# One batch loop with stages becomes an unrolled pipeline over 64 tiles

## The reference

```python
x = x + _layernorm(_L0_attn_ref(_layernorm(x), ...))
x = x + _layernorm(_L0_ffn_ref(_layernorm(x), ...))
```

```python
scores = jnp.einsum('bqhd,bkhd->bhqk', q, k) / np.sqrt(HD)
scores = jnp.where(causal[None, None], scores, jnp.finfo(scores.dtype).min)
attn = jax.nn.softmax(scores, axis=-1)
...
topv, topi = jax.lax.top_k(probs, K)        # K = 2 of 8 experts per row
a = jax.nn.silu(g) * u                      # g, u: per expert, 256 -> 512
out = jnp.clip(residual + moe_out, -100.0, 100.0)
```

## Time and profile before

| | us |
|---|---|
| median of 3 runs | 4165.04 (4164.26 to 4166.23) |
| the profiled execution's own time | 4157.04 |
| its span | 4155.2 |
| TensorE, VectorE, ScalarE, GpSimd busy | 3078.5, 2298.0, 1675.9, 1106.6 |
| mean granted clock of TensorE | 0.873 of full |
| first turn of the batch loop | 31 to 434 |
| experts and final pass | from 3221.6 to the end |

### The profile page before, as it was taken

One profiled execution on the slowest core, in us unless ns is written; L12 is line 12 of the kernel. 1 busy time (PEld: TensorE's weight loads), 2 busy tenths in 40 slices (PEclk: granted clock), 3 DMA queues, 4 the chain that ended last, 5 costly groups with the idle time before them and its releaser, 6 DMA issues. The chain is left out here.

```text
span 4155.2 us, 54042 instructions
## 1 busy us (share of the span) xinstructions
PE 3078.5 (74%) x17636; PEld 1799.8 (43%) x17637; DVE 2298.0 (55%) x4488; ACT 1675.9 (40%) x3702; POOL 1106.6 (27%) x972
## 2 busy tenths in 40 slices
PE   5588558765965696579657955885587599999991
PEld 3444434343434443443444343444343366666660
DVE  4775567466837672866386557755675122222225
ACT  2456254525542554256335624562455122222223
POOL 6310630072016202420332053106200222222222
PEclk9789789887988898889788988997789799999995
DMA  1000000000000000000000000000000533333335
GB/s 55 11 11 12 22 21 2 13 20 21 2 30 3 21 2 32 0 21 2 32 1 21 2 32 11 12 12 22 11 2 11 185 55 55 55 61 56 55 53 167
DMA packets 85960, 125.57 MB, mean 30 GB/s; under 512 B 11600, under 2 KB 70864, under 8 KB 83664
## 3 DMA queue, kind: packets, MB, share of 16 engines
q1 hardware_dynamic: 59216, 85.40, 6.5%
q0 software_dynamic: 26496, 37.01, 5.0%
HBM read 58.23 MB, written 63.36 MB: 29 GB/s over the span
## 5 line engine op out<-in xcount | busy, mean ns | idle before, releaser
L660 ACT ACTIVATE PR<-SP_ 128x512 f32<-128x512 f32 (+3 forms) x1536 | 693.8, 489 | 457.8 <-PE SP_ L1241 310.9
L925 DVE TENSOR_REDUCE NM<-MX 128x1 f32<-128x128 f32 (+7 forms) x1024 | 733.9, 752 | 231.2 <-PE MX L1210 221.0
L421 POOL DMA_INDIRECT scratch_xs<-FX,SLOT x128 | 123.7, 967 | 1467.1 <-issue 1465.5
L439 POOL TENSOR_TENSOR work<-QK,VS 128x2048 f32<-128x2048 f32 x128 | 466.6, 3670 | 136.4 <-DVE QK L774 136.2
L1238 PE MATMUL SP_<-work,KST 99*128 99x512 bf16 (+3 forms) x1536 | 469.0, 333 | 44.1 <-ACT PR L660 32.2
L1208 PE MATMUL MX<-KST,work 96*128 96x512 bf16 (+3 forms) x1536 | 442.8, 353 | 70.0 <-DVE NM L925 58.5
L1503 POOL DMA_INDIRECT scratch_h<-Y,XG x136 | 210.6, 1548 | 617.1 <-DVE Y L1566 522.9
L1544 DVE TENSOR_TENSOR AG<-UB,SL 128x512 f32<-128x512 f32 x136 | 94.0, 691 | 476.3 <-PE UB L1583 476.3
L1254 PE MATMUL OA<-PR,V 128*32 128x512 f32 (+3 forms) x3072 | 327.3, 498 | 3.3 <-ACT PR L660 3.3
L1521 ACT ACTIVATE SL<-GB 128x512 f32<-128x512 f32 x136 | 81.2, 597 | 602.3 <-PE GB L1583 602.3
L818 DVE TENSOR_REDUCE AT<-work 128x256 f32<-128x4096 f32 x64 | 282.9, 4420 | 2.2
(11 more groups left out here) (253 smaller groups left out, 5092.7 us busy)
## 6 DMA issues: line engine op xcount, KB each, us to landing
XG<-scratch_xs SPq DMA_DIRECT2D x136, 130.0 KB, 2.1
X<-in_L_attn_x SPq DMA_DIRECT2D x8, 1024.0 KB, 5.6
scratch_x<-X SPq DMA_DIRECT2D x8, 1024.0 KB, 3.9
scratch_h<-A SPq DMA_DIRECT2D x8, 1024.0 KB, 3.9
X<-scratch_x SPq DMA_DIRECT2D x16, 512.0 KB, 4.0
HH<-scratch_h SPq DMA_DIRECT2D x16, 512.0 KB, 4.5
out<-X SPq DMA_DIRECT2D x16, 512.0 KB, 3.1
wg<-in_L_ffn_Wg SPq DMA_DIRECT2D x1, 4096.0 KB, 16.7
```

Source lines behind the costliest of these rows:

```text
L439: sg["prod1"].by(pool.tensor_tensor(P1[t % 2][:, i * hh * D:(i + 1) * hh * D].rearrange("p (h e d) -> p h e d", h=hh, e=HD), QK[:, t % 3, ...
L660: sg["exp"].by(act.activation(PR[:, n % 8, q0:512], SP_[:, n % 2, q0:512], ACT.Exp))
L925: sg["mx"].by(dve.tensor_reduce(NM[:, qt, h:h + 1], src, AX.X, ALU.max, negate=True))
```

## The change

The loop and the meeting points are gone. Each engine's program is one unrolled list: 87 periods after a short lead-in, 24 slots in each. In period p, slot i, an engine does one step of the front stages for tile p, or p - 1, p - 2, p - 6, p - 7, p - 8, and of the closing stages for tile p - 17 to p - 22. Between these, `share(p, i)` deals out steps of the second attention, from period 12 on: 32 per period in four periods, then 16 per period in four, and so on. The attention's own order (chunks of queries, one after the other over all batches, with a table of maxima in units of a quarter step) is a generator that each engine resumes.

With it, buffers get smaller: tiles of one batch become rings (x 10 tiles, AT 3, A2 6, HS 12), most work tiles single. PSUM is dealt out anew: GA, GB and SUM are one bank each, shared by all front and closing steps; scores keep two banks, maxima have a ring of two, in which the turned output also takes its place. A row maximum over more than 512 keys is now two pieces and two reductions. Key products, query products and query sums are halved (8 heads each). The copy of the attention's output (OT) moves from VectorE to ScalarE. Roots and reciprocals are one power on GpSimd. Norm coefficients are computed per tile, routing per four tiles (it was eight), x is loaded per tile. At the end the program clears its semaphores.

The diff, cut to its core:

```diff
+RX = 10
+RAT = 3
+RA2 = 6
+RHS = 12
+RK = 3
+RV = 4
...
-        XN = sb("XN", [P, 2, D])
-        XT = sb("XT", [P, 2, FC, P])
-        EX = sb("EX", [P, 2, 2 * D])
-        QK = sb("QK", [P, 3, 2 * D])
-        VS = sb("VS", [P, 2, D])
-        SQ = sb("SQ", [P, 2, D])
+        XN = sb("XN", [P, D])
+        XT = sb("XT", [P, FC, P])
+        EX = sb("EX", [P, 2 * D])
+        QK = sb("QK", [P, 2, 2 * D])
+        VS = sb("VS", [P, D])
+        P1 = sb("P1", [P, 2, H * D // 2])
+        P2 = sb("P2", [P, H * D // 2])
+        KT = sb("KT", [P, D])
+        SQ = sb("SQ", [P, D])
+        AT = sb("AT", [P, RAT, D])
...
-        MX = ps("MX", [P, 2, 2, 512])
         SP_ = ps("SP_", [P, 2, 512])
+        GA = ps("GA", [P, 512])
+        GB = ps("GB_", [P, 512])
+        SUM = ps("SUM", [P, 512])
         SP_ = ps("SP_", [P, 2, 512])
+        MX = ps("MX", [P, 2, 512])
         OA = ps("OA", [P, 512])
...
+                first = FIRST_STEP[u]
+                if g == 0:
+                    late = (2.8, 1.6)[c]
+                    spans = [(first - (9, 6.5)[c], first - late)] * 3 + [(first - late, first - 0.8)]
+                    done = first - 0.8
+                else:
+                    done = first - (2.0, 3.0)[c]
+                    begin = max(FIRST_STEP[HKV * j] - 0.6, done - (4, 9)[c])
+                    spans = [(begin, done)] * CH
...
+        SLOTS = 24
+        START = 12 * SLOTS + 4
+        LAST_PERIOD = TT + 23
+        LAST_BACK = TT + 12
+        def share(p, i):
+            if p * SLOTS + i < START:
+                return 0
+            n = 32 if p % 8 < 4 else 16
+            return (i + 1) * n // SLOTS - i * n // SLOTS
...
-            with sp.Fori(0, B - 1) as b:
-                batch(b, True)
+                    do(pool.tensor_tensor(xco[:, 1:2], xco[:, 0:1], powers[:, 0:1], ALU.pow))
...
+                    if t >= 1:
+                        need("heads_summed", 2 * t - 1 + half)
+                    hh = H // 2
+                    r = slice(half * hh * HD, (half + 1) * hh * HD)
+                    sg["prod1"].by(pool.tensor_tensor(
...
-                        sg["ot"].by(dve.tensor_copy(OT[:, :], OA[:, :]))
+                        sg["ot"].by(act.activation(OT[:, :], OA[:, :], ACT.Copy))
...
+                def query_products(t, half):
+                    need("kv", t + 1)
+                    need("attn", 2 * t + half)
+                    r = slice(half * hh * HD, (half + 1) * hh * HD)
+                    sg["prod2"].by(dve.tensor_tensor(
+                        products, QK[:, t % 2, r].rearrange("p (h e) -> p h e", e=HD).unsqueeze(2).broadcast_to(shape),
+                        KVP.rearrange("p (d e) -> p d e", e=HD).unsqueeze(1).broadcast_to(shape), ALU.mult))
+                def query_sums(t, half):
+                    need("prod2", 2 * t + half + 1)
+                    if t >= RAT and half == 0:
+                        need("a2", t - RAT + 1)
+                    r = slice(half * hh * HD, (half + 1) * hh * HD)
+                    sg["attn"].by(dve.tensor_reduce(AT[:, t % RAT, r].rearrange("p (h d) -> p h d", d=HD), products, AX.X, ALU.add))
...
-                for t in range(NT + 3):
-                    if t < NT:
-                        elu(t)
-                    if 2 <= t <= NT + 1:
-                        attended(t - 2)
+                        if i == 0 and have(p - 1):
+                            query_sums(p - 1, 1)
+                        if i == 1 and have(p - 8):
+                            parts(p - 8, 0)
+                        if i == 2 and have(p):
+                            elu(p)
+                        if i == 2 and have(p - 8):
+                            parts(p - 8, 1)
+                        if i == 3 and have(p - 8):
+                            parts(p - 8, 2)
...
+                            flatten(p - 17)
+                        if i in (20, 22) and have(p):
+                            query_products(p, (i - 20) // 2)
+                        if i == 21 and have(p):
+                            query_sums(p, 0)
+                        if p * SLOTS + i == START:
+                            next(back)
+                        for _ in range(share(p, i)):
+                            next(back, None)
...
+                def bank_b():
+                    need("fT", sg["tpf"].n)
+                    need("vcopy", sg["qkv"].n // 2)
+                    need("hT", sg["tph"].n)
...
+                    j, g, c = unit(u)
+                    if index >= 2:
+                        need("mx", index - 1)
+                    need("qts", 2 * (CH * j + i + 1) - (1 if h + G * g < 8 else 0))
+                    need("kts", CH * j + i + 1)
+                    n = min(512, (CH * c + i + 1) * P - 512 * part)
+                    keys = j - c + part
+                    last = part == c
+                    out = MX[:, index % 2, 0:n]
+                    m = pe.matmul(out, QST[0:MROW, j % 2, g * G + h, i * P:(i + 1) * P], KST[0:MROW, keys % RK, g, 0:n],
...
+                for p in range(-1, LAST_PERIOD):
+                    for i in range(SLOTS):
+                        if i == 0 and have(p - 18):
+                            transpose_flat(p - 18)
+                        if i in (1, 2) and have(p):
+                            project(p, i == 2)
+                        if i == 4 and have(p - 18):
+                            route(p - 18)
...
+                        if i == 20 and have(p):
+                            turn_sums(p)
+                        if p * SLOTS + i == START:
+                            next(back)
+                        for _ in range(share(p, i)):
+                            next(back, None)
```

More of the change, by code:

```diff
@@ L162, in attention_kernel @@
+        cmv = sb("cmv", [P, 2])
+        cco = sb("cco", [P, 2, 8])
+        MS = sb("MS", [P, H])
+        R16 = sb("R16", [P, 2, H])
+        row = sb("row", [P, 3])
+        rms = sb("rms", [P, 3])
+        LG = sb("LG", [P, CH, E])
+        top = sb("top", [P, CH, 8])
+        topi = sb("topi", [P, CH, 8], U32)
         below = sb("below", [P, P])
@@ L287, in dve_plan @@
-        def dve_plan():
-            plan = max_plan()
-            yield from plan[0]
-            for k, (u, kt) in enumerate(steps()):
-                actions = plan[k + 1]
-                first = len(actions) // G
-                yield from actions[:first]
-                if kt == 0 and u >= 1:
-                    yield "out", u - 1
-                yield from actions[first:]
-                if kt == 1 and u >= 1:
-                    yield "ctx", u - 1
-            yield "out", len(UNITS) - 1
-            yield "ctx", len(UNITS) - 1
@@ new lines, in attention_kernel, with unit, length, steps @@
+        NU = TT // CH * HKV
+        NSTEPS = TT // CH // 2 * HKV * (CH + 2 * CH)
+        def unit(u):
+            j = u // HKV
+            return j, u % HKV, j % 2
+        def length(u):
+            return CH * (1 + unit(u)[2])
+        FIRST_STEP = [0]
+        for u in range(NU):
+            FIRST_STEP.append(FIRST_STEP[-1] + length(u))
+        assert FIRST_STEP[-1] == NSTEPS
+        def steps():
+            for u in range(NU):
+                for kt in range(length(u)):
+                    yield u, kt
@@ new lines, in last_step, with max_plan @@
+        def last_step(j):
+            return FIRST_STEP[HKV * (j + 1)]
+        def max_plan():
+            timed = []
+            for u in range(NU):
+                j, g, c = unit(u)
[8 more added lines that the diff above has]
+                    spans = [(begin, done)] * CH
+                for i in range(CH):
+                    cells = [("piece", u, h, i, part) for h in range(G) for part in range(c + 1)]
+                    lo, hi = spans[i]
+                    if g == 0 and i == CH - 1:
+                        n0, n1, total = 0, len(cells), len(cells)
+                    elif g == 0:
+                        n0, n1, total = i * len(cells), (i + 1) * len(cells), 3 * len(cells)
+                    else:
+                        n0, n1, total = i * len(cells), (i + 1) * len(cells), CH * len(cells)
+                    for n, cell in zip(range(n0, n1), cells):
+                        timed.append((lo + n * (hi - lo) / total, cell))
+                timed.append((done, ("parts", u)))
+                timed.append((done + 0.3, ("rows", u)))
+                if u >= 1:
+                    timed.append((first + 1.6, ("turn", u - 1)))
+            timed.sort(key=lambda x: x[0])
+            buckets = [[] for _ in range(G * NSTEPS + 1)]
+            index = 0
+            for time, (kind, *args) in timed:
+                at = max(0, 1 + int(time * G)) if time >= 0 else 0
+                if kind == "parts":
+                    buckets[at].append((kind, *args, None))
+                else:
+                    buckets[at].append((kind, *args, index))
+                    index += 1
+            return buckets, index
```

(23 more changed lines are left out.)

1989 lines of the change are left out of this document (988 added, 1001 removed), and 5 rows, old and new, of the table names.

## The result

The changed kernel takes 4242.01 us (median of 4 runs, 4234.28 to 4250.62) beside 4164.94 us of the kernel before on the same chip: ratio 1.0184, 95% interval 1.0172 to 1.0196. It is slower by 1.8%; the forecast was 3790, and 4242 lies above its range (3540 to 4110). The profiled execution has a span of 4235.6 us.

A forecast was written before the change was run, and what follows sets the result against it. First and last stages wait for hand-overs, the second attention for TensorE. Start 29, fill 276, periods 12 to 63 2166, then 310 and 57 sum to 2838; block change 7; experts start 377 us earlier: about 3790 us, range 3540 to 4110.

The forecast's parts named there:

- heavy: Period with 32 steps of the second attention: forecast 47.8 us, with 22.6 us of attention on TensorE.
- light: Period with 16 steps of the second attention: forecast 36.4 us, with 12.7 us of attention on TensorE.
- VectorE's stretch: From VectorE's products in slot 20 to elu of the next tile in slot 2: 15.6 us heavy, 13.1 light.
- The lock: VectorE's cast after elu is held until GpSimd's first product ends: +3.7 us per period, bounds 0 and 7.3.
- The rival without a lock: VectorE's casts and GpSimd's long products pass each other: -192 us, 3600 us; chance 0.22.
- TensorE's stretch: TensorE's work left over after VectorE's stretch, 29.0 and 21.5 us; at 93.9% busy, 30.9 heavy and 22.9 light.
- a head start: TensorE begins its stretch two maximum pieces ahead: -2.4 us in heavy periods, -3.3 in light ones.
- the clock: TensorE, half idle in VectorE's stretch, runs 16 us per period at half speed: +416, about 4205 us; chance 0.13.
- slot-by-slot coupling: TensorE's stretch 80% busy rather than 94%, through waits in 24 slots: +5.4 and +4.0 us, 4030 us; chance 0.14.
- The fill: Periods 0 to 11, without attention: a single-buffered chain per tile of 23 us, 276 us in all.
- The powers: Five GpSimd powers per tile, bounded by 0 and 3.6 us, put at no cost on the path.
- The drain: Periods 64 to 75, without new tiles, TensorE-bound: 310 us; then last four tiles, routing and scatters: 57 us.

The follow-up runs named there:

- the pairs of runs: Heavy periods of three runs, each beside its base kernel: 0.3 to 0.45 us less busy time per us less at the low clock in the middle stretch.
- e13: Changed kernel plus two zero-adding filler matmuls ahead of each maximum piece in slots 20 to 23 and 0 to 5: 4230.83 us against 4242.
- e3: Changed kernel with the logits copy out of bank SUM moved from VectorE to ScalarE: 4153.35 us against 4242.
- e6: Changed kernel with GpSimd's power done for one head root instead of 16, result not valid: 4204.15 us against 4242.
- experiment 5: The same run as e6: changed kernel with GpSimd's power done for one head root instead of 16: 4204.15 us against 4242.
- e14: Kernel with elu behind parts, logits on ScalarE, later second sums, spread products, later norm_heads (3916), plus two zero-adding fillers ahead of pieces: 3936.07 us.
- e10: One filler matmul at the start of slots 20 to 23, 0 and 1, on a kernel with elu behind parts, logits on ScalarE, later second sums (3937): 4004.58 us.

## Why the prediction was wrong

Its sum, term by term, up to the start of the experts:

| | forecast | measured | difference |
|---|---|---|---|
| start | 29 | 31.8 | +3 |
| periods 0 to 11 | 276 | 333.2 | +57 |
| periods 12 to 62 (24 heavy, 27 light) | 2130 | 2453.2 | +323 |
| period 63 to the experts | 410 | 485.9 | +76 |
| experts start | 2845 | 3304.1 | +459 |

**VectorE's stretch** was right: 15.3 + 0.7 for elu = 16.0 us where 15.6 was forecast, light 13.6 beside 13.1.

**The lock** was right in cause and size: the cast is held for 3.67 us, and with the subtraction ahead of it 4.1 us pass from elu's end to its end where 3.7 stood. The Trainium skill, page "SBUF — State Buffer", section "Who interferes with whom", has the second of the two engines held for the whole instruction of the first, and reductions never. The trace agrees with both: the cast takes 3.67 us in 56 of 64 tiles and 0.33 in the last eight, which no product accompanies, and a reduction (L1042) that starts at 1708.49 beside GpSimd's product takes its usual 0.69 us. The rival without a lock falls.

**TensorE's stretch** is the step that failed: "The steady second attention is 93.9% busy at clock 1.00, so 30.9 and 22.9 us", minus 2.4 and 3.3. It came to 34.0 and 25.1 instead of 28.5 and 19.6, +5.5 us in both kinds of period. Its work was right in size: 29.7 busy less 3.6 lost by the clock is 26.1 where 26.6 was forecast, light 18.7 where 18.2. That was partly luck. In VectorE's stretch TensorE did what was forecast (9.0 and 6.6 us at full clock), so its work of a whole period is 35.1 and 25.9 us by the same reckoning, not 38.0 and 28.1; the 2.4 and 3.3 us taken off for a head start, of which the trace shows little (0.0 and 1.1 us busy while the cast is held), made up for it. Two other parts were not right:
- *The clock.* The 1.00 came from a stretch in which TensorE never pauses. In the new order its stretch begins behind a pause, and the earlier trace rows had shown a clock of 0.56 and 0.61 after one. At 3.6 and 2.9 us that is 24 x 3.6 + 27 x 2.9 = 165 us, by the 0.3 to 0.45 of the pairs of runs 100 to 150. That 7.2 and 5.8 us were worked at the low clock is shown; that this much would come back with it is an estimate and not shown, as no run lifted it there alone. Waits that take its place, the rival of e13, are not ruled out.
- *Idle time.* 4.3 and 3.5 us where 6% gave 1.9 and 1.4: 24 x 2.4 + 27 x 2.1 = 114 us. The named part is the wait for the logits copy: taking it away is worth 89 us of the kernel (e3), but 24 x 1.2 + 27 x 0.4 = 40 of these 114 us; the others are spread over waits for maxima, for scores and for the bank SUM. The prediction counted the bank ring of the maxima and overlooked that the users of the bank SUM (head sums, turn_sums, second_layer, route) are ordered one behind the other, with VectorE's place in the queue between them.

The remaining 0.8 us per period are the 0.4 each of VectorE's stretch and the lock, 41 us. 165 + 114 + 41 = 320 of 323. The sum closes because busy time, idle time and length are of one trace; it doesn't test the price of the clock.

So neither rival was whole. The slow one, "the clock", had the right mechanism, and the low clock came to 16.0 us per period, as it supposed. But "8 us of work are lost" counted every one of them: the price was at most about 3 us a period in the middle stretch and little in VectorE's own. By itself it would have given at most 3790 + 165. The rival "slot-by-slot coupling" had +5.4 and +4.0 for idle time; 2.4 and 2.1 came. The forecast gave them a chance each, as if one excluded the other; they came together, and with fill and drain.

**The fill.** "23 us" was right for periods 0 to 4 (21.7 to 24.0), wrong for 8 to 11 (32.9 to 36.2), where the steps of tile p - 8 join. The powers, bounded by 0 and 3.6 us for five, cost 2.92 us for the 16 heads alone and 6.1 us for all six of a tile, outside the bounds: the price was taken from a product's width, while a power of 16 elements takes three quarters of the time of a product of 2048 (2.92 and 3.74 us). e6 makes 14 us of the 57. Ten of the add_gains products (L901) are held by GpSimd's second product, by the same lock (shortest, median, longest ns):

```profile
L901 DVE TENSOR_TENSOR A<-A,AT x64: 412/504/3527, 84.4 to 2926.7; 128x256 f32<-128x256 f32 x64
```

Which of them closes the chain was not isolated.

**The drain**, 76 us more, was lost ahead of its last tiles. By the logits copies (L969, one per period) periods 64 to 67 take 154 us where 124 were forecast, 68 to 71 take 105 instead of 80, 72 to 75 take 112 instead of 106; period 63 is a steady one, with a steady period's loss. From there to the experts it is 63 us where 64 were forecast, the four last tiles at 8.1 to 8.4 instead of 7.5 included. The clock is 0.82 in this part too; no run takes its loss apart. The block change is as forecast: GpSimd idles 7.67 us behind its last scatter.

What the forecast got wrong as a whole was the sign: the steady period had to lie under 49.8 us by more than fill and drain take. With 41.8 it did; with 48.1 it gained 84 us and paid 173.

## What to carry to other kernels

Cost a new software pipeline as steady period, fill and drain, and write down for each of the three what it is before; a gain of 3% per tile does not pay for twelve periods of fill in 64. Take an engine's rate from a stretch with the same pauses in front of it as the new order will have, and list every user of a shared PSUM bank with the engine that has to free it. What a step releases matters as much as what it costs: putting the small steps of parts ahead of elu, not behind it, was worth 168 us, and moving an 8-column copy to the idle engine 89.

## What the hardware showed beyond that

- GpSimd's power takes 0.57 us for 1 element per partition, 0.88 for 3 and 2.92 for 16, by the rows in experiment 5: about 0.16 us per further element. A product of 2048 elements takes 3.74.
- The granted clock can be raised without any gain. 0.843 became 0.869 with the time the same within the noise (e13), and from 0.884 it went to 0.920 at 21 us more (e14).
- A filler's wait costs more than its matmuls: six of 0.2 us each, behind a wait for ScalarE to free a bank, made periods of the fill 2 us longer (e10).
